# A two-layer mixture-of-experts block on one core: a new order ahead of the first step, tanh in place of exp and sigmoid, and an in-SBUF copy of the first mixing matrices

## The chip, the cores and the metric

One NeuronCore of a Trainium2 chip runs the whole program. The metric is the device time of one execution in microseconds (us); the median of three executions of the kernel before is 399.89 us (398.08 to 400.11). The engines are named PE (TensorE, matmuls), ACT (ScalarE), DVE (VectorE), POOL (GpSimd) and SP (SyncE, which here only issues transfers).

## The reference, cut to what matters

Two layers, each a mixing of the 32 channels of a sample followed by a feed-forward layer with eight low-rank experts, of which each token uses two; x is [128, 32, 512]. The first mixing is a grouped convolution of nine taps; the second is a 32x32 matrix for each sample, a softmax-weighted sum of eight matrices, where the weights come from a small network on `cond`.

```python
def _L0_ffn_ref(x, W_base, b_base, W_router, A, B):
    base = xf @ W_base.T + b_base
    rw, sel = jax.lax.top_k(xf @ W_router.T, 2)
    rw = jax.nn.softmax(rw, axis=-1)
    lora = einsum('ter,te,eor->to', einsum('td,erd->ter', xf, A), w, B) * 2.0
    return base + lora

def _L1_cond_ref(x, embedding, W0, b0, W1, b1, W2, b2, weight, bias_k):
    h = gelu(embedding @ W0 + b0); h = gelu(h @ W1 + b1)
    att = jax.nn.softmax(h @ W2 + b2, axis=-1)
    return einsum('boi,bih->boh', einsum('bk,koi->boi', att, weight), x) + att @ bias_k

x = x + _L0_ffn_ref(_L0_cond_ref(x, cond_128, ...), ...)
x = x + _L1_ffn_ref(_L1_cond_ref(x, cond_128, ...), ...)
```

## The kernel before

The 128 samples are worked on in 32 tiles of four samples, 128 tokens (sample and channel) of 512 values each. Every number that goes into a large matmul is split into a high part (`fp32r`, made by an ACT copy) and a low part (the rest, made by a subtraction on DVE or POOL), and each product is three matmuls: high x high, high x low, low x high (`SPLITS`). The weights of both layers (`wa`: experts' A, router and the first half of the base; `wb`: its second half; `lb_w`: experts' B) are loaded once and split once.

For tile t the first layer is `conv(t)` on PE, `conv_out` on DVE (adds a bias, gives `y0`), `turn0` (four transposes on PE), `turned0` on ACT and DVE (high and low parts of `yT`), `first_product(0,t)`, `choose` and `gate` on DVE with `weigh` on ACT between them (the two best experts and their weights), `turn_hw`, `second_product`, `b_product`, and `middle` on DVE, which writes `x1`. The second layer is `mix_product(t)` (PE; `x1` against `mix_part`, the split mixing matrices of the tile's four samples), `save_cross`/`sum_mixed`/`turned1`, then `first_product(1,t)` and so on, and `result` on DVE. The loop is a software pipeline: `step(t)` does the first layer of tile t, the convolution of tile t+1 and the second layer of tiles t-1 and t-2.

Nothing schedules this but the order in which the instructions of each engine are written, and semaphores between engines. Each engine has one queue in order, so an instruction that waits holds back all behind it on that engine. SP's queue of transfers works in the same way.

Ahead of `step(1)` the kernel splits weights, runs the small network (two Gelus, a softmax with exp) and makes `mix_nat`, all mixing matrices as rows of one sample each. `mix` holds them block-diagonally, four samples to a tile; the blocks are brought there by writing `mix_nat` to a scratch tensor in HBM and reading it back with four transfers (L256 to L262). PE's own order ahead of the first step is at L390 to L453. While PE waits for other engines there it runs matmuls on zeros, `keep_busy` (L384): ten at the start, and

```python
            conv(0)
            kernel_scores()
            turn0(0)
            keep_busy(4)
            turn_probabilities()
            keep_busy(2)
            mixing_setup()
            first_product(0, 0)
```

On ACT three activation tables are loaded: Gelu at the start (L495), exp for the softmax (L506), sigmoid for `weigh` (L513). ACT's order is at L495 to L507 and L585 to L601, DVE's at L814 to L832, POOL's at L903 to L920.

## Time and profile before

| | |
|---|---|
| three executions | 398.08, 399.89, 400.11 us |
| the profiled execution | 400.4 us, span 398.6 us (first to last instruction) |
| PE busy | 387.8 us, 97% of the span |
| DVE, POOL, ACT busy | 70%, 57%, 52% |
| mean granted clock of PE | 0.996 of full speed |
| chain that ended last | PE 91%, DVE 5%, DMA 1% |

The span is what the trace covers; the time of the same execution is 1.8 us longer. Shares of busy time are means over the span: the 40 us ahead of and in the first steps have other limits than the loop. The trace has for each instruction its start, its duration and, in brackets, how long its engine had stood idle before it and what ended that. PE's clock has two levels, 1.2 and 2.4 GHz; the profile gives the granted level as 0.50 or 1.00.

### The profile page before, as it was taken

What the parts mean: (1) busy time and instruction counts of PE and PEld (TensorE: products, weight loads), DVE (VectorE), ACT (ScalarE), POOL (GpSimd) and SP (SyncE); (2) the same over time, 40 slices, a digit from 0 to 9 for tenths busy, and PEclk for the clock granted to TensorE, in tenths of its full rate; (3) what the DMA queues carried; (4) which work ended last, traced back from release to release, by engine and by line L of the source; (5) the groups of instructions that cost most, each with busy time, mean ns of one, the idle gap of its engine ahead of it and who ended that gap; (6) DMA issues with size and microseconds to landing.
All of it is one profiled execution on the core that took longest, in us unless ns stands there. A gap on an engine that the chain in (4) does not pass through costs nothing.

```text
span 398.6 us, 9113 instructions
## 1 busy us (share of the span) xinstructions
PE 387.8 (97%) x2789; PEld 377.5 (95%) x2789; DVE 280.8 (70%) x982; ACT 207.8 (52%) x529; POOL 226.7 (57%) x199
## 2 busy tenths in 40 slices
PE   7979999999999999999999999999999999999985
PEld 6659999999999999999999999999999999999975
DVE  2786876777667677766777676677777767767764
ACT  3846455555455555544555555455555545555441
POOL 3386756555666555556656555665655566655550
PEclk9998999999999999999999999999999999999999
DMA  7871212122221212222112122211212222121101
GB/s 257 297 142 55 76 31 81 56 79 79 79 79 38 68 57 75 79 79 79 54 52 70 62 79 79 79 59 47 79 53 79 79 79 77 37 72 53 56 27 54
DMA packets 19677, 31.04 MB, mean 78 GB/s; under 512 B 5904, under 2 KB 5936, under 8 KB 19664
## 3 DMA queue, kind: packets, MB, share of 16 engines
q1 hardware_dynamic: 19664, 30.89, 25.1%
q8 instruction: 6, 0.10, 0.1%
q14 instruction: 7, 0.06, 0.0%
...
## 4 chain that ended last, share of the span: by engine, by line
PE 91%; DVE 5%; DMA 1%; issue 1%; ACT 0%; POOL 0%; SPq 0%; DVEq 0%; ACTq 0%
PE ps_out L331 33%; PE ps_out L343 22%; PE ps_conv L299 11%; PE ps_out L363 11%; PE ps_mix L377 5%; PE ps_t L311 3%; PE ps_mix L380 2%; DMA pack<-in_pack 1%; PE ps_t L350 1%; DVE wb L625 1%; DVE yT L625 1%; PE ps_out L350 1%; DVE y L774 1%; DVE lb_w L641 0%; DVE x L767 0%
## 5 line engine op out<-in xcount | busy, mean ns | idle before, releaser
L331 PE MATMUL ps_out<-wa,yT 128*128 128x392 f32 x768 | 152.5, 345 | 1.4 <-ACT yT L476 0.7
L331 PEld LDWEIGHTS ps_out<-wa,yT 128*128 128x128 f32 x768 | 132.2, 188 | 4.8 <-DVE yT L625 1.8
L879 POOL TENSOR_TENSOR x_part<-x,x_part 128x512 fp32r<-128x512 f32 x31 | 40.1, 1295 | 116.4 <-ACT x_part L476 116.4
L343 PE MATMUL ps_out<-wb,yT 128*128 128x256 f32 x768 | 105.6, 287 | 0.2 <-DVE wb L625 0.2
L343 PEld LDWEIGHTS ps_out<-wb,yT 128*128 128x128 f32 x768 | 97.2, 191 | 0.4 <-issue 0.4
L476 ACT ACTIVATE yT<-ps_t 64x256 fp32r<-64x256 f32 x128 | 48.5, 379 | 29.3 <-PE ps_t L311 26.9
L363 PE MATMUL ps_out<-lb_w,hwT 128*128 128x256 f32 x384 | 59.5, 289 | 1.3 <-ACT hwT L476 0.7
L892 POOL TENSOR_TENSOR x1b<-x,base_bias 128x512 f32<-128x512 f32 x31 | 40.1, 1294 | 28.4 <-DVE res L752 28.4
L625 DVE TENSOR_TENSOR yT<-ps_t,yT 64x256 fp32r<-64x256 f32 x128 | 53.7, 420 | 3.0
L513 ACT ACTIVATE wts<-top 128x1 f32<-128x1 f32 x128 | 30.4, 284 | 46.5 <-DVE top L716 46.5
L299 PE MATMUL ps_conv<-x_part,conv_w 128*128 128x256 f32 x384 | 52.2, 286 | 0.0
L363 PEld LDWEIGHTS ps_out<-lb_w,hwT 128*128 128x128 f32 x384 | 49.7, 189 | 2.6 <-ACT hwT L476 1.2
L299 PEld LDWEIGHTS ps_conv<-x_part,conv_w 128*128 128x128 f32 x384 | 49.3, 192 | 0.0
L864 POOL TENSOR_TENSOR x_part<-x_raw,x_part 128x520 fp32r<-128x520 f32 x31 | 40.5, 1308 | 12.0 <-ACT x_part L476 12.0
L885 POOL TENSOR_TENSOR base_bias<-passed,bias 128x512 f32<-128x512 f32 x32 | 41.8, 1306 | 4.0 <-ACT passed L539 4.0
L875 POOL TENSOR_TENSOR xb<-x_tok,bias 128x512 f32<-128x512 f32 x32 | 41.8, 1305 | 0.0
L476 ACT ACTIVATE x_part<-x_raw 128x520 fp32r<-128x520 f32 x32 | 20.5, 640 | 34.9 <-PE ps_conv L299 34.9
L752 DVE TENSOR_TENSOR res<-ps_out,x1b 128x512 f32<-128x512 f32 x31 | 21.4, 691 | 20.5 <-PE ps_out L363 20.5
L377 PE MATMUL ps_mix<-mix_part,x_part 128*128 128x256 f32 x128 | 31.4, 323 | 1.4 <-issue 1.4
L476 ACT ACTIVATE yT<-ps_mix 128x512 fp32r<-128x512 f32 x32 | 19.1, 598 | 24.0 <-DVE ps_mix L787 23.1
L625 DVE TENSOR_TENSOR hwT<-ps_out,hwT 128x128 fp32r<-128x128 f32 x32 | 9.3, 290 | 30.6 <-ACT hwT L476 30.6
L380 PE MATMUL ps_mix<-mix_part,x_part 128*128 128x128 f32 x128 | 28.6, 224 | 0.0
...
## 6 DMA issues: line engine op xcount, KB each, us to landing
...
x_tok<-in_x_tok SPq DMA_DIRECT2D x32, 256.0 KB, 2.6
out<-res SPq DMA_DIRECT2D x31, 256.0 KB, 2.0
...
lb_raw<-in_lb SPq DMA_DIRECT2D x2, 256.0 KB, 5.8
bias<-in_bias SPq DMA_DIRECT2D x2, 256.0 KB, 5.8
...
```

Source lines behind the costliest of these rows:

```text
L299: last = mm(ps_conv[:, h * SPT * NB:(h + 1) * SPT * NB], conv_w[:, wp, h, shift, :], x_part[dp][:, h, :, shift:shift + NB], start=(n == 0 ...
L331: last = mm(out_banks(y, t)[:, 0, 0:AR + DH], yT[y][dp][:, k, :], wa[y][:, wp, k, :], start=(n == 0 and k == 0), stop=(n == len(SPLITS) - ...
L343: last = mm(out_banks(y, t)[:, 1, OUT], yT[y][dp][:, k, :], wb[y][:, wp, k, :], start=(n == 0 and k == 0), stop=False, skip_group_check=True)
L363: last = mm(out_banks(y, t)[:, half, OUT], hwT[y][dp][:, :], lb_w[y][:, wp, half * DH:(half + 1) * DH], start=False, stop=(n == len(SPLITS ...
L377: mm(ps_mix[:, b, c:c + 2 * P], x1_part[HI][:, k * P:(k + 1) * P], mix_part[:, :, :].rearrange("p a b -> p (a b)"), start=True, stop=False ...
L476: return nc.scalar.activation(dst, src, ACT.Copy)
L625: return v.tensor_tensor(dst, src, hi, ALU.subtract)
L864: g.tensor_tensor(x_part[LO][:, :, :, :], x_raw[:, :, :, :], x_part[HI][:, :, :, :].bitcast(F32), ALU.subtract).then_inc(s["xl"], 1)
L875: g.tensor_tensor(xb[:, :], x_tok[:, :], bias[0][:, :], ALU.add).then_inc(s["xb"], 1)
L879: g.tensor_tensor(x1_part[LO][:, :], x1[:, :], x1_part[HI][:, :].bitcast(F32), ALU.subtract).then_inc(s["x1l"], 1)
L885: g.tensor_tensor(base_bias[:, :], passed[:, :], bias[1][:, :], ALU.add).then_inc(s["bb"], 1)
L892: g.tensor_tensor(dst[:, :], x1[:, :], base_bias[:, :], ALU.add).then_inc(s["x1b"], 1)
```

## The change

- **PE's order.** Nine matmuls on zeros in place of ten, `conv(0)` directly behind them and ahead of the small network; the other six matmuls on zeros are gone. `turn_probabilities` stands inside `first_product(0,0)` behind its first four matmuls, `conv(1)` inside it ahead of its last four, `mixing_setup` behind it.
- **ACT's order.** `wa` of layer 0 is made in two halves around the second Gelu, `wa` of layer 1 ahead of the first `weigh`; both halves of `mix_nat` are copied by ACT (one was DVE's); `save_sums`, `pass_bias(0)`, `high_wb(1)` and `high_lb(1)` move from `step(1)` to the part ahead of it. `split_mix(0)` stands ahead of `split_x1(0)`.
- **One table.** The softmax takes e^x = 2/(1 - tanh(x/2)) - 1, so DVE has six small operations on `att` between the scores and the product with `own` where it had two and the scores' maximum. `weigh` takes 1 + tanh(x/2): a small copy `half_top` ahead of each pair, with a semaphore between, for every tile of both layers. `lb_w` takes half the scale.
- **POOL.** It subtracts the second half of layer 0's `wa` (was DVE's), and forms `xb` of tile 0 ahead of the column sums.
- **SP.** `lb0` and `x` of tile 1 are loaded ahead of `kern`, the second layer's `lb1` and `bias1` ahead of `mix_nat`. Four transfers inside SBUF bring the first tile's blocks from `mix_nat` to `mix`; then the scratch tensor is written and the other tiles' blocks are read back. ACT waits for the first four ahead of `split_mix(0)`, for the others in `step(1)`.

PE ahead of the first step, before: `ps_out<-x_part` are the matmuls on zeros, `ps_conv` the convolution, `ps_t` the transposes of `y0`, `att_m` and `att_mT` the softmax.

```order
L388 MATMUL ps_out<-x_part 128x512 x10
L393 MATMUL ps_mix<-pack 128x128
L396 MATMUL ps_mix<-pack 128x128 x2
L399 MATMUL ps_mix<-hid,pack 128x128
L299 MATMUL ps_conv<-x_part,conv_w 128x256 x12
L403 MATMUL ps_mix<-pack,hid 128x8
L311 MATMUL ps_t<-pack,y 128x128 x4
L388 MATMUL ps_out<-x_part 128x512 x4
L408 MATMUL ps_mix<-pack,att_m 32x128
L388 MATMUL ps_out<-x_part 128x512 x2
L415 MATMUL ps_mix<-att_mT,bk_sb 128x128
L418 MATMUL ps_mix<-kern_sb,att_mT 128x512
```

And in the changed kernel:

```order
L399 MATMUL ps_out<-x_part 128x512 x9
L307 MATMUL ps_conv<-x_part,conv_w 128x256 x12
L404 MATMUL ps_mix<-pack 128x128
L407 MATMUL ps_mix<-pack 128x128 x2
L410 MATMUL ps_mix<-hid,pack 128x128
L319 MATMUL ps_t<-pack,y 128x128 x4
L414 MATMUL ps_mix<-pack,hid 128x8
L342 MATMUL ps_out<-wa,yT_0 128x392 x4
L419 MATMUL ps_mix<-pack,att_m 32x128
L342 MATMUL ps_out<-wa,yT_0 128x392 x4
L307 MATMUL ps_conv<-x_part,conv_w 128x256 x12
L342 MATMUL ps_out<-wa,yT_1 128x392 x4
```

The convolution came up, four products of `first_product(0,0)` stand ahead of the softmax's transpose, and between the transposes of `y0` and `second_product` no matmul on zeros is left.

ACT ahead of the first step, before, from the first Gelu on (`hid`):

```order
L501 ACTIVATE hid<-ps_mix,pack 128x128
L503 ACTIVATE hid<-ps_mix,pack 128x128
L476 ACTIVATE wa<-wa_raw 128x1568
L506 ACT_TABLE_LOAD
L506 ACTIVATE att,att_s<-att,att_s 128x8
L476 ACTIVATE yT_0<-ps_t 64x4x64 x4
L476 ACTIVATE wb<-wb_raw 128x1024
L493 ACTIVATE lb_w<-lb_raw 128x512
L476 ACTIVATE x_part<-x_raw 128x520
L476 ACTIVATE mix_nat<-ps_out 128x512
L513 ACT_TABLE_LOAD
L513 ACTIVATE wts<-top 128x1 x2
```

And in the changed kernel:

```order
L589 ACTIVATE hid<-ps_mix,pack 128x128
L485 ACTIVATE wa<-wa_raw 128x784
L592 ACTIVATE hid<-ps_mix,pack 128x128
L485 ACTIVATE wa<-wa_raw 128x784
L485 ACTIVATE yT_0<-ps_t 64x4x64 x2
L507 ACTIVATE att<-att 128x8
L485 ACTIVATE yT_0<-ps_t 64x4x64 x2
L485 ACTIVATE x_part<-x_raw 128x520
L485 ACTIVATE wb<-wb_raw 128x1024
L502 ACTIVATE lb_w<-lb_raw 128x512
L485 ACTIVATE wa<-wa_raw 128x784 x2
L512 ACTIVATE half_top<-top 128x2
```

The two table loads behind the Gelus are gone. The softmax's operation now stands between the two pairs of `yT` copies, and no longer ahead of both.

POOL ahead of the first step, before (`k_sums`, `k_sum` are layer 1's column sums):

```order
L903 MEMSET mix 128x4096
L904 MEMSET ones 128x128
L864 ISA
L864 TENSOR_TENSOR x_part<-x_raw,x_part 128x520
L908 TENSOR_TENSOR k_sums<-wa_raw 128x2x392
L911 TENSOR_TENSOR k_sums<-wb_raw 128x2x256
L914 TENSOR_TENSOR k_sum<-k_sums 128x648
L875 TENSOR_TENSOR xb<-x_tok,bias 128x512
L879 TENSOR_TENSOR x_part<-x,x_part 128x512
L869 TENSOR_TENSOR mix_part<-mix,mix_part 128x128
```

And in the changed kernel:

```order
L925 MEMSET mix 128x4096
L926 MEMSET ones 128x128
L928 ISA
L928 TENSOR_TENSOR wa<-wa_raw,wa 128x784
L886 TENSOR_TENSOR x_part<-x_raw,x_part 128x520
L897 TENSOR_TENSOR xb<-x_tok,bias 128x512
L935 TENSOR_TENSOR k_sums<-wa_raw 128x2x392
L938 TENSOR_TENSOR k_sums<-wb_raw 128x2x256
L941 TENSOR_TENSOR k_sum<-k_sums 128x648
L891 TENSOR_TENSOR mix_part<-mix,mix_part 128x128
L901 TENSOR_TENSOR x_part<-x,x_part 128x512
```

A subtraction on half of `wa` came in at the front, `xb` moved ahead of the column sums, and `mix_part` ahead of `x_part<-x`.

The diff, cut to its core:

```diff
@@ block.sync: behind load_weights(0)
+            sp.dma_start(lb_raw[0][:, :], d["lb0"]).then_inc(l_lb[0], 16)
+            load_x(1)
             sp.dma_start(kern_sb[:, :], d["kern"]).then_inc(l_kern, 16)
             sp.dma_start(bk_sb[:, :], d["bk"]).then_inc(l_kern, 16)
...
+            sp.wait_ge(mix_zero, 1)
             sp.wait_ge(mix_nat_ready, 2)
+            for n in range(SPT):
+                sp.dma_start(mix[n * C:(n + 1) * C, n, :],
+                             mix_nat[n:n + 1, :].rearrange("p (i o) -> p i o", o=C)).then_inc(mix_first, 16)
             sp.dma_start(d["scratch"], mix_nat[:, :]).then_inc(mix_stored, 16)
-            load_x(2)
             sp.wait_ge(mix_stored, 16)
-            sp.wait_ge(mix_zero, 1)
             for j in range(SPT):
-                sp.dma_start(mix[j * C:(j + 1) * C, j::SPT, :],
-                             d["scratch"][j::SPT, :].rearrange("t (i o) -> i t o", o=C)).then_inc(mix_loaded, 16)
+                sp.dma_start(mix[j * C:(j + 1) * C, SPT + j::SPT, :],
+                             d["scratch"][SPT + j::SPT, :].rearrange("t (i o) -> i t o", o=C)).then_inc(mix_loaded, 16)
@@ block.tensor
-            keep_busy(10)
+            keep_busy(9)
+            conv(0)
...
-            conv(0)
+            turn0(0)
             kernel_scores()
-            turn0(0)
-            keep_busy(4)
-            turn_probabilities()
-            keep_busy(2)
+            first_product(0, 0, before_cross=turn_probabilities, before_low=lambda: conv(1))
             mixing_setup()
-            first_product(0, 0)
-            conv(1)
             second_product(0, 0)
@@ block.scalar
-            nc.scalar.activation(att[:, 1, :], att[:, 0, :], ACT.Exp, bias=att_s[:, 0:1],
-                                 accum_out=att_s[:, 1:2]).then_inc(mlp_act, 1)
+                act.wait_ge(mlp_dve, 3)
+                nc.scalar.activation(att[:, 2, :], att[:, 1, :], ACT.Tanh).then_inc(mlp_act, 1)
...
                 act.wait_ge(s["top"][y], t + 1)
+                nc.scalar.activation(half_top[y][:, :], top[y][:, 0:2], ACT.Copy, scale=0.5).then_inc(s["half"][y], 1)
+                act.wait_ge(s["half"][y], t + 1)
                 for k in range(2):
-                    nc.scalar.activation(wts[y][:, k:k + 1], top[y][:, 1 - k:2 - k], ACT.Sigmoid, scale=-1.0,
-                                         bias=top[y][:, k:k + 1]).then_inc(s["wts"][y], 1)
+                    nc.scalar.activation(wts[y][:, k:k + 1], top[y][:, 1 - k:2 - k], ACT.Tanh, scale=-0.5,
+                                         bias=half_top[y][:, k:k + 1]).then_inc(s["wts"][y], 1)
...
             turned0(0, 0)
+            probabilities()
             turned0(0, 1)
+            split_x(1)
             high_wb(0)
             high_lb(0)
-            split_x(1)
...
+            act.wait_ge(mix_first, 16 * SPT)
+            split_mix(0)
             split_x1(0)
-            act.wait_ge(mix_loaded, 16 * SPT)
-            split_mix(0)
+            save_sums()
+            pass_bias(0)
+            high_lb(1)
             split_x(2)
@@ block.vector: probabilities()
+                v.tensor_scalar(att[:, 1, :], att[:, 2, :], -1.0, 1.0, ALU.mult, ALU.add).then_inc(mlp_dve, 1)
...
+                v.reciprocal(att[:, 3, :], att[:, 1, :]).then_inc(mlp_dve, 1)
...
+                v.tensor_scalar(att[:, 0, :], att[:, 3, :], 2.0, -1.0, ALU.mult, ALU.add).then_inc(mlp_dve, 1)
...
+                v.tensor_reduce(att_s[:, 1:2], att[:, 0, :], AX.X, ALU.add).then_inc(mlp_dve, 1)
@@ block.gpsimd
+            pool.wait_ge(wa_hi[0], 2)
+            g.tensor_tensor(wa[0][:, LO, LAST_KS, :], wa_raw[0][:, LAST_KS, :], wa[0][:, HI, LAST_KS, :].bitcast(F32),
+                            ALU.subtract).then_inc(wa_lo[0], 1)
             split_x(1)
+            pool.wait_ge(l_bias[0], 16)
+            form_xb(0)
...
+            split_mix(0)
             split_x1(0)
-            split_mix(0)
```

## Rows read from the trace of the kernel before

**Rows 1.** Page, part 1: busy us, share of the span and instructions of each engine
```profile
PE 387.8 (97%) x2789; PEld 377.5 (95%) x2789; DVE 280.8 (70%) x982; ACT 207.8 (52%) x529; POOL 226.7 (57%) x199
```

**Rows 2.** Chain of waits in order of time, in the loop: start us, us, what
```profile
52.84 2.15 PE ps_out L331 x12
...
58.12 1.43 PE ps_conv L299 x12
...
64.39 2.14 PE ps_out L331 x12
```

**Rows 3.** Timeline, PE ahead of step 1: start us, us, instruction, count [idle before]
```profile
1.46 4.64 PE L388 MATMUL ps_out<-x_part 128*128 128x512 f32 x10 [1.46 <-DVE x_part L645]
...
6.87 0.80 PE L393 MATMUL ps_mix<-pack 128*128 128x128 f32 x2 [0.77 <-DMA pack<-in_pack]
...
8.64 2.46 PE L299 MATMUL ps_conv<-x_part,conv_w 128*128 128x256 f32 x12
...
11.95 0.66 PE L311 MATMUL ps_t<-pack,y 128*128 128x128 f32 x4 [0.73 <-DVE y L774]
...
14.13 0.48 PE L415 MATMUL ps_mix<-att_mT,bk_sb 32*128 32x128 f32 x2
...
16.27 1.70 PE L331 MATMUL ps_out<-wa,yT 128*128 128x392 f32 x8
```

**Rows 4.** Timeline, ACT ahead of step 1
```profile
10.81 1.28 ACT L506 ACT_TABLE_LOAD   x1
...
12.20 0.30 ACT L506 ACTIVATE att<-att,att_s 128x8 f32<-128x8 f32 x1
...
12.64 1.59 ACT L476 ACTIVATE yT<-ps_t 64x256 fp32r<-64x256 f32 x4
...
21.02 0.48 ACT L513 ACTIVATE wts<-top 128x1 f32<-128x1 f32 x2 [2.74 <-DVE top L716]
```

**Rows 5.** Timeline, DVE and POOL: operations with two SBUF inputs, alone and side by side
```profile
12.08 0.96 DVE L625 TENSOR_TENSOR wa<-wa_raw,wa 128x784 fp32r<-128x784 f32 x1
...
16.44 1.31 POOL L864 TENSOR_TENSOR x_part<-x_raw,x_part 128x520 fp32r<-128x520 f32 x1 [12.04 <-ACT x_part L476]
...
17.71 1.86 POOL L908 TENSOR_TENSOR k_sums<-wa_raw 128x784 f32<-128x784 f32 x1
...
18.13 2.53 DVE L625 TENSOR_TENSOR wb<-wb_raw,wb 128x1024 fp32r<-128x1024 f32 x1
```

**Rows 6.** Timeline, PE and DVE: the way to step 1
```profile
22.38 0.33 PE L350 MATMUL ps_out<-pack,hw 128*128 128x128 f32 x1
...
25.25 0.69 DVE L767 TENSOR_TENSOR x<-ps_out,xb 128x512 f32<-128x512 f32 x1 [1.04 <-POOL xb L875]
```

**Rows 7.** Timeline, SP and PE: the way to the first mixing product
```profile
19.82 2.47 SPq L261 DMA_DIRECT2D mix<-scratch  x4
...
30.04 0.36 PE L377 MATMUL ps_mix<-mix_part,x_part 128*128 128x256 f32 x1 [1.37 <-issue]
```

**Rows 8.** DMA issues: transfers, KB each, median us from issue to landing
```profile
out<-res SPq DMA_DIRECT2D x31, 256.0 KB, 2.0
...
mix<-scratch SPq DMA_DIRECT2D x4, 128.0 KB, 3.5
```

**Rows 9.** Stretches: us, busy us of each engine (x), granted clock, DMA share, GB/s
```profile
31.00:34.00 3.00, 3.00 (x16) 3.00 (x16) 1.04 (x3) 2.67 (x7) 0.74 (x2) 0.50 0.30 89
...
34.00:35.00 1.00, 1.00 (x9) 1.00 (x9) 0.52 (x1) 1.00 (x2) 1.00 (x2) 0.85 0.00 0
```

**Rows 10.** Timeline, the last tile: ACT, DVE and PE
```profile
388.50 0.60 ACT L476 ACTIVATE yT<-ps_mix 128x512 fp32r<-128x512 f32 x1 [0.94 <-PE ps_out L343]
...
392.90 0.18 DVE L731 TENSOR_TENSOR ps_out<-ps_out,wts 128x16 f32<-128x16 f32 x1
...
393.67 0.33 PE L350 MATMUL ps_t<-pack,hw 128*128 128x128 f32 x1
```

**Rows 11.** Timeline, ACT in the loop
```profile
55.24 0.48 ACT L513 ACTIVATE wts<-top 128x1 f32<-128x1 f32 x2 [1.27 <-DVE top L716]
```

158 lines of the change are left out of this document (84 added, 74 removed).

## The prediction, made before the changed kernel ran

> **What bounds the kernel now.** Start with the busy shares [rows 1]: PE is busy for 97% of the span, the next engine for 70%. So only two things make the kernel shorter: less work on PE, or fewer stretches in which PE stands still or runs at its lower clock. The chain of waits in order of time [rows 2] says where those stretches are not. From one `first_product(0,t)` to the next it takes 64.39 - 52.84 = 11.55 us, all of it PE, step after step. The change removes nothing from PE in the loop, so the loop can't gain; it can only lose. What is left is the part ahead of the loop, and the last tile. There I read the timeline, engine by engine.
>
> Four things are to be seen in it. First, PE runs at 1.2 GHz at the start: `conv(0)`, twelve matmuls, takes 2.46 us [rows 3], the same form 1.43 later [rows 2]. Second, `step(1)` begins when `x1` of tile 0 is written, at 25.25 + 0.69 = 25.94, and DVE had stood 1.04 for `xb` there [rows 6]. Third, the mixing product waits: PE is idle for 1.37 us until 30.04 [rows 7]. Fourth, right after that the granted clock stands at 0.50 (the 1.2 GHz level) from 31 to 34, and at a mean of 0.85 in the next microsecond, which is 0.3 us more [rows 9]. 3.3 us at half the clock lose 1.65 us of PE's work. The stall and the low clock together, 3.0 us, are what this change could win at most in step 1.
>
> **The sum.** It is made against the profiled execution (400.4 us, its span and 1.8 us around it), which is 0.5 above the median of the three.
>
> *Convolution first.* Nine matmuls on zeros instead of ten end at 1.46 + 0.9 x 4.64 = 5.6, and `conv(0)` starts there and not at 8.64: 3.0 earlier. But the products for its bias, which lay ahead of it (6.87 to 8.64, 1.8 us [rows 3]), now lie between it and `y0`. So the transposes of `y0`, which ended at 11.95 + 0.66 = 12.61, end some 1.2 earlier, at 11.4.
>
> *Table loads.* The two removed cost nothing. The first ended at 12.09 and its exp ran at 12.20, once DVE had the maximum; after the second ACT still stood 2.74 for `top` [rows 4]. The Trainium skill (ScalarE: Activation LUTs, "What ACT_TABLE_LOAD costs") puts each switch of table set at about 2.66 us with its drain. By that the change would win 5.3 us; the rows show 1.28 for a load, and none of it on the path.
>
> *The softmax.* This is where the change loses. DVE's operations on the scores and `wa` now meet POOL's subtraction on half of `wa`. How such a meeting goes is shown by [rows 5]: POOL's 128x784 sum ran from 17.71 to 19.57; DVE's 128x1024 subtraction, started at 18.13, ended at 20.66, which is 1.09 after POOL's end, while DVE alone takes 0.96 for 784 columns, so about 1.2 for 1024. It did nothing until POOL was done. The Trainium skill (SBUF — State Buffer, "Who interferes with whom") has this as a lock on a shared pair of ports, held for a whole instruction, and says that `tensor_scalar` can be caught as well. The first agrees with the rows; no row of before shows the second. POOL's half starts behind ACT's, at about 11, and takes 1.86: until 12.9. Then DVE subtracts its own half (0.96, to 13.9), and does five small operations at about 0.2 (an estimate: ACT's on the same 128x8 takes 0.30 [rows 4]): 14.9. The product with `own` has two SBUF inputs again and may meet `split_x(1)`, 1.31 on POOL. So `att_m` is written between 15.1 and 16.4; I take 16.0, nearer to the blocked end, as in the row of the same kind. Before, it was used by 13.5. Of the `yT` copies (1.59 [rows 4]) the second pair waits for the tanh and ends between 13.3 and 14.2, where before they ended at 14.23.
>
> *PE from there.* Behind `att_m`, PE has its transpose (0.2), eight of the first product's twelve matmuls (two thirds of 2.15), `conv(1)` 1.43, the mixing set-up (14.13 to 16.27, 2.1 [rows 3]) and the second product, as many matmuls of the same form as a convolution, 1.43: 6.6. From 16.1 that ends at 22.7, and `turn_hw` was at 22.38 [rows 6]: 0.3 late at full clock. The four products done early win 0.7, the set-up that moved behind costs that back and more.
>
> *The clock.* Between 11.4 and 16.1 PE now has about 1.0 us of work. The matmuls on zeros that filled this stretch are gone. Before, 1.37 us of idleness were followed by a fall for 3.3 us; here nearly 4 of 4.7 us are idle. I expect the fall, and for as long, in the dense work behind: 1.65. `turn_hw` is then at 24.35.
>
> *To `x1`.* Before, it took 25.94 - 22.38 = 3.56, of which 1.04 was for `xb`. That wait goes, as `xb` is formed ahead of the column sums. DVE has half of layer 1's `wa` and a pair of `yT` in front of `x1` instead, in part beside PE. Take 2.8: `x1` at 27.2, 1.2 late.
>
> *To the mixing product.* The last kernel product ends 1.43 ahead of `turn_hw`, at 22.9. ACT's last copy of `mix_nat` takes 0.60 (as its copy of the same size in [rows 10]): 23.5. Four issues took 2.47 us [rows 7], so the last goes out 1.85 after the first, at 25.4. The trace has no transfer inside SBUF; the nearest are a store with 2.0 to landing and the scratch reads with 3.5 [rows 8], whose 128-byte pieces the new ones share while they are a thirty-second of the size. I take the middle, 2.75, and keep both ends: the blocks land at 28.1 (27.4 to 28.9). Behind this wait on ACT stand `split_mix(0)` and, newly, `split_x1(0)`, and behind that POOL's low part: 0.3 + 0.6 + 1.3 = 2.2. The product starts at 30.35 (29.6 to 31.1), 0.3 late. PE's idleness ahead of it shrinks nevertheless, because `step(1)` starts late too: 27.25 + 2.15 = 29.4, so 0.95 and not 1.37. I take this as not enough for a second fall: 1.65 won.
>
> *The loop.* `half_top` adds one operation of some 0.3 us ahead of each pair of `weigh`. ACT had stood 1.27 us there [rows 11], and PE waits for nothing in the step: zero. The cover is that slack; without it each step would cost up to 0.3, 32 steps some 10 us.
>
> *The last tile.* Here nothing covers it. DVE takes the weights at 392.90, and PE turns the result at 393.67, as soon as it is there [rows 10]: 0.3 late. A tile earlier ACT's `yT` at 388.50 waited for PE as well as for the chain behind `weigh`: 0.1 more. Together 0.4.
>
> Sum: +0.3 - 1.65 + 0.4 = -0.95, so 400.4 - 0.95 = 399.45, about **399.5 us**.
>
> **The rivals.** *The clock holds in the front* (chance 0.2). For it: PE came through gaps of 0.7 there before [rows 3]. Against it: the gaps are now several times that. Then `x1` comes at about 26.0 and the product at 29.4: -0.65 - 1.65 + 0.4 = -1.9, 398.5; with DVE's small operations not blocked another 0.9, 397.6.
>
> *The clock falls again at the mixing product, and the kernel is slower* (0.2). The place is ACT's wait for the four transfers, with `split_x1(0)` queued behind it. It decides from an idle stretch of about 1.4, which is reached if landing takes 3.2 and not 2.75. Then nothing of the 1.65 is won: up to +1.1 late and +0.4, 401.9. If the low clock in the front also lasts twice as long, 1.65 more: 403.5. I put this case at 402.3.
>
> *The tables count after all* (0.05): by the skill's price per switch, 5.3 us less, 395.1. The waits behind both loads speak against it.
>
> *All of it is hidden* (0.05): DVE's queue, not PE, sets `x1` in both orders, and the late start eats what step 1 wins: 400.4.
>
> **How the numbers follow.** My forecast has 0.5 and by its own bounds (landing 2.0 to 3.5, `att_m` 15.1 to 16.4) reaches from 398.5 to 400.8. About 0.5%, 2.0 us, can be told from no change here, so faster means below 397.9, slower above 401.9. Faster: a third of the first rival, the table rival, and a tail of my own: 0.17. Slower: somewhat over half of the second rival, and a tail: 0.14. Between: 0.69. The range from 397.5 to 402.5 leaves out the ends of both large rivals and the tables, 0.15 or so.
>
> **What would show it.** Right: one table load in ACT's rows; PE mostly idle between 11.5 and 16, and a granted clock of 0.50 behind that; DVE's `att` or `wa` rows longer than alone, ending after a POOL row; an idle stretch under 1.2 ahead of the mixing product, and 1.00 from 30 to 36; 11.55 per step; `turn_hw` of the last tile 0.3 later behind `top` than before. Wrong: a granted clock of 1.00 from 12 to 24, `att_m` before 14, or the four blocks landing within 3 us of `mix_nat` with PE waiting all the same.

## The result, and the profile after

The changed kernel took **400.39 us** (median of 20 executions, 399.01 to 401.47), the kernel before, beside it, 398.61 (20 executions, 397.33 to 400.33). The ratio is 1.0039, with a 95% interval from 1.0027 to 1.0050: 1.1 to 2.0 us slower. That is inside the predicted range and under the 0.5% that I had called no change, but it is on the other side: I had forecast 0.4 less than the median shown and 0.95 less than the profiled execution.

One thing has to be known before the two traces are compared. The profiled execution of before, 400.40, is longer than each of the 20 just named; the profiled one of after, 399.01, is the shortest of its 20. So the two traces say 1.4 us faster where the times say 1.6 slower. Each step below is therefore read in several traces of each kernel.

Page of the changed kernel, part 1, which answers to [rows 1]: ScalarE has gained 11 us (two more `half_top` operations per step), PE has lost 4. One table load is left of three.

```profile
PE 383.9 (97%) x2782; PEld 374.5 (94%) x2782; DVE 281.2 (71%) x986; ACT 218.8 (55%) x593; POOL 226.8 (57%) x200
```

Timeline of the changed kernel, PE from the convolution to the first mixing product (start us, us, instruction, count [idle before]), which answers to [rows 3, 6, 7]:

```profile
5.11 1.72 PE L307 MATMUL ps_conv<-x_part,conv_w 128*128 128x256 f32 x12
...
8.92 0.66 PE L319 MATMUL ps_t<-pack,y 128*128 128x128 f32 x4 [0.86 <-DVE y L796]
...
13.51 1.65 PE L342 MATMUL ps_out<-wa,yT 128*128 128x392 f32 x4 [3.44 <-ACT yT L485]
15.51 0.40 PE L419 MATMUL ps_mix<-pack,att_m 128*32 128x128 f32 x1 [0.35 <-DVE att_m L694]
...
23.49 0.27 PE L361 MATMUL ps_out<-pack,hw 128*128 128x128 f32 x1
...
27.36 2.41 PE L342 MATMUL ps_out<-wa,yT 128*128 128x392 f32 x12 [1.07 <-DVE x L789]
29.61 0.28 PE L388 MATMUL ps_mix<-mix_part,x_part 128*128 128x256 f32 x1
```

The 3.44 us gap at 10 to 13.5 is where the fillers had been. The mixing product has no idle time ahead of it any more (1.37 in [rows 7]), and the stretch from 31 to 34 has its full clock, where [rows 9] had 0.50. The low clock lies ahead of step 1 instead, and not only here: the 42 executions of the changed kernel in this document all have a mean granted clock of 0.989 to 0.995. Stretches of the changed kernel (us, busy us of PE, PEld, DVE, ACT, POOL, granted clock, DMA share, GB/s):

```profile
11.00:18.00 7.00, 4.14 (x14) 3.65 (x15) 6.67 (x14) 4.71 (x9) 5.18 (x4) 0.53 1.01 366
18.00:19.00 1.00, 1.00 (x9) 1.00 (x8) 1.00 (x1) 0.00 (x0) 1.00 (x2) 0.85 0.80 273
31.00:34.00 3.00, 3.00 (x25) 2.98 (x24) 1.98 (x6) 1.57 (x5) 3.00 (x3) 1.00 1.00 130
```

DVE's small operations of the softmax, timeline of the same kernel. The first `tensor_scalar` on `att` took 1.81 and ended with POOL's half of `wa` (10.45 + 1.83); the second, alone, took 0.16. `att_m` was held in the same way by `split_x(1)` on POOL at 14.10.

```profile
10.50 1.81 DVE L678 TENSOR_SCALAR att<-att,att_s 128x8 f32<-128x8 f32 x1
12.23 0.96 DVE L641 TENSOR_TENSOR wa<-wa_raw,wa 128x784 fp32r<-128x784 f32 x1
13.11 0.16 DVE L684 TENSOR_SCALAR att<-att 128x8 f32<-128x8 f32 x1
...
14.14 1.31 DVE L694 SCALAR_TENSOR_TENSOR att_m<-att,att_s,pack 128x32 f32<-128x32 f32 x1
```

The table that the rest is read from is worked out from the timelines: the start of the first mixing product, the intervals from the first matmul of one mixing product to that of the next (step 1, step 2, and the mean of 26 in the loop), what follows the last of the 32, the span, and the time around the span. The lines below the second are executions of the experiments.

| trace | first mixing product | step 1 | step 2 | loop | after the last | span | around it |
|---|---|---|---|---|---|---|---|
| before, profiled | 30.0 | 12.83 | 11.96 | 11.545 | 12.8 | 398.6 | 1.8 |
| after, profiled | 29.6 | 11.72 | 12.21 | 11.532 | 13.0 | 397.2 | 1.8 |
| c_before | 29.6 | 11.48 | 11.95 | 11.544 | 12.8 | 396.8 | 1.8 |
| c_after | 29.2 | 11.73 | 12.18 | 11.533 | 13.1 | 396.9 | 2.5 |
| c_after2 | 30.9 | 11.72 | 12.16 | 11.533 | 13.1 | 398.5 | 2.7 |
| e_nohalf | 30.0 | 10.75 | 12.01 | 11.533 | 13.6 | 397.0 | 1.8 |
| e_wadve | 28.8 | 11.70 | 12.16 | 11.533 | 13.1 | 396.4 | 2.4 |
| e_bhold | 31.2 | 11.48 | 11.96 | 11.544 | 12.9 | 398.5 | 1.9 |

### The profile page after: what moved, and what is told of

Same layout as the page of the kernel before. It is cut to its first block, busy times and chain, and to the rows that moved or that the text cites. A ratio compares the mean times of both kernels' runs of the same rounds, so it can differ in the third digit from the quotient of the medians.

```text
span 397.2 us, 9172 instructions
## 1 busy us (share of the span) xinstructions
PE 383.9 (97%) x2782; PEld 374.5 (94%) x2782; DVE 281.2 (71%) x986; ACT 218.8 (55%) x593; POOL 226.8 (57%) x200
## 4 chain that ended last, share of the span: by engine, by line
PE 88%; DVE 5%; ACT 2%; issue 2%; DMA 2%; POOL 0%; SPq 0%; DVEq 0%; ACTq 0%
PE ps_out L342 33%; PE ps_out L354 21%; PE ps_conv L307 11%; PE ps_out L374 11%; PE ps_mix L388 5%; PE ps_t L319 3%; PE ps_mix L391 2%; DMA wa_raw<-in_wa 2%; PE ps_t L361 1%; PE ps_out L361 1%; DVE yT L641 1%; DVE x L789 1%; ACT yT L485 0%; DVE att L678 0%; DVE lb_w L653 0%
## 5 line engine op out<-in xcount | busy, mean ns | idle before, releaser
L354 PE MATMUL ps_out<-wb,yT 128*128 128x256 f32 x768 | 104.2, 285 | 0.0
L354 PEld LDWEIGHTS ps_out<-wb,yT 128*128 128x128 f32 x768 | 95.8, 189 | 0.8 <-issue 0.8
L485 ACT ACTIVATE yT<-ps_t 64x256 fp32r<-64x256 f32 x128 | 48.5, 379 | 28.4 <-PE ps_t L319 26.0
L914 POOL TENSOR_TENSOR x1b<-x,base_bias 128x512 f32<-128x512 f32 x31 | 40.1, 1295 | 27.8 <-DVE res L774 27.8
L512 ACT ACTIVATE half_top<-top 128x2 f32<-128x2 f32 x64 | 12.5, 195 | 36.7 <-DVE top L738 36.7
L515 ACT ACTIVATE wts<-top,half_top 128x1 f32<-128x1 f32 x128 | 30.7, 287 | 2.1
L388 PE MATMUL ps_mix<-mix_part,x_part 128*128 128x256 f32 x128 | 31.2, 321 | 0.0
```

The lines of the kernel that those rows point to most:

```text
L354: last = mm(out_banks(y, t)[:, 1, OUT], yT[y][dp][:, k, :], wb[y][:, wp, k, :], start=(n == 0 and k == 0), stop=False, skip_group_check=True)
L388: mm(ps_mix[:, b, c:c + 2 * P], x1_part[HI][:, k * P:(k + 1) * P], mix_part[:, :, :].rearrange("p a b -> p (a b)"), start=True, stop=False ...
L485: return nc.scalar.activation(dst, src, ACT.Copy)
L914: g.tensor_tensor(dst[:, :], x1[:, :], base_bias[:, :], ALU.add).then_inc(s["x1b"], 1)
```

## The experiments

### Both kernels once more

`c_before` is the kernel before, `c_after` and `c_after2` are the changed one, with no edit.

> The kernel before, unchanged, to have span and granted clock of each of its executions. Theory A (the clock: before loses 1.65 us to a low clock in step 1 in part of its executions only, the change loses to a low clock in its front in every one): the executions fall into two groups some 1.7 apart, the longer ones with a mean granted clock of about 0.996 and the shorter ones with 1.000. Rival B (before's spread has nothing to do with the clock): clock the same in long and short executions. Rival C (the loss of the change lies outside the span): time less span is 1.8 in all executions here, where the change has 1.8 to 3.1.

> The changed kernel unchanged, beside the kernel before on the same chip. Theory A (the measured +1.6 us is the kernel's own): span near 398.0 with the low clock of the front in every execution (mean granted clock 0.989 to 0.994), and a time outside the span that varies between 1.8 and 3.0 with a median near 2.5, against 1.8 for the kernel before; ratio 1.003 to 1.005. Rival B (the +1.6 us came of the chip or the sample): span and time within 0.5 us of the kernel before, time outside the span 1.8.

> The changed kernel unchanged, once more on the chip of this call. Theory A: time outside the span 1.8 to 3.0 with a median above 2.1, median span 397.5 to 398.1, ratio to the kernel before 1.002 to 1.006; in its trace the low clock lies ahead of step 1 and the first two steps take 11.7 and 12.2 us. Rival B (the first two traces were of short executions and are not typical): a span near 398.0 with one of the first two steps longer by 0.5 us or more, or the front.

Measured: `c_before` 398.44, ratio 0.9997 [0.9981, 1.0013]; `c_after` 399.99, ratio 1.0039 [1.0023, 1.0056]; `c_after2` 400.54, ratio 1.0036 [1.0017, 1.0054]. The loss is the kernel's own, and it has two parts. On the chip of `c_after2` the mean span was 398.14 against 397.03 for the kernel before (1.1), and the time around the span 2.39 against 1.80 (0.6); on the chip of `c_after` 397.82 against 397.08, and 2.34 against 1.80.

`c_before` also shows what the profiled execution of before had hidden. Timeline of `c_before`, PE, and the stretch from 31 to 34:

```profile
29.60 0.36 PE L377 MATMUL ps_mix<-mix_part,x_part 128*128 128x256 f32 x1 [1.37 <-issue]
```

```profile
31.00:34.00 3.00, 3.00 (x25) 3.00 (x25) 1.43 (x3) 2.97 (x7) 1.10 (x1) 1.00 0.34 89
```

The stall is the same 1.37 us as in [rows 7]. The clock after it stayed at 1.00, and step 1 took 11.48, not 12.83. So the fall cost 1.35 us where it happened.

Of the theories for `c_before`, C held: the time around the span was 1.76 to 1.84 in all twelve executions. A held in part. Beside `c_before`, `c_after`, `c_after2` and `e_bhold` 117 executions of the kernel before can be compared, and in 60 of these its mean granted clock was 0.996 or less. These 60 had spans longer by 0.6, 1.2, 1.2 and 1.2 us in the mean than the others of the same chip, but the two groups overlap. Where the low clock lay in them is not shown, since only one execution of a run has a trace.

`c_after2` shows a longer front. Timeline, PE, and stretches:

```profile
5.46 2.42 PE L307 MATMUL ps_conv<-x_part,conv_w 128*128 128x256 f32 x12
...
13.65 1.25 PE L342 MATMUL ps_out<-wa,yT 128*128 128x392 f32 x4 [2.89 <-ACT yT L485]
...
24.74 0.27 PE L361 MATMUL ps_out<-pack,hw 128*128 128x128 f32 x1
...
30.87 0.28 PE L388 MATMUL ps_mix<-mix_part,x_part 128*128 128x256 f32 x1
```

```profile
11.00:14.00 3.00, 0.35 (x2) 0.38 (x3) 2.86 (x7) 1.87 (x6) 1.43 (x1) 1.00 1.05 338
14.00:21.00 7.00, 6.26 (x25) 5.42 (x23) 6.14 (x10) 3.24 (x5) 6.67 (x5) 0.51 0.68 244
```

In the profiled execution the low clock began at about 11 and ran in part over the gap, where PE had nothing to do. Here it began at 14, when the gap was over, and fell on work throughout: `turn_hw` 24.74 instead of 23.49, for the same low clock of some 7 us. Its length differs too. In `c_after`, stretches:

```profile
11.00:13.60 2.60, 0.00 (x0) 0.00 (x0) 2.56 (x4) 1.22 (x5) 1.49 (x1) 1.00 1.08 319
13.60:17.00 3.40, 2.94 (x9) 2.45 (x10) 3.17 (x9) 3.16 (x5) 2.69 (x3) 0.50 0.99 396
17.00:18.00 1.00, 1.00 (x10) 1.00 (x9) 0.94 (x3) 0.54 (x1) 1.00 (x1) 0.98 0.93 345
```

There it was 3.4 us, and the first mixing product came at 29.2. Mean granted clocks of 0.994 or 0.995, as in this execution, are rare: 4 of the 42. Where the low clock begins and how long it lasts differs from one execution to the next.

### The clock's fall in step 1 of the kernel before, alone

`e_bhold` fills PE's 1.37 us stall of step 1 in the kernel before.

```
                 first_product(0, t)
+                if isinstance(t, int) and t == 1:
+                    pe.wait_ge(s["x1h"], 1)
+                    for _ in range(6):
+                        mm(ps_mix[:, 0, :], x1_part[HI][:, 0:P], x1_part[HI][:, :], start=True, stop=True)
                 mix_product(t - 1)
```

> The kernel before with six filler products in step 1 of the loop, where TensorE waits for the low half of x1 (1.37 us idle ahead of the first mixing product), nothing else. This takes out by itself the fall of the clock that the prediction priced at 1.65 us. Theory A (that fall is what separates the longer executions of the kernel before, some 1.5 us longer and a third of them, from the shorter ones): the first step takes 11.5 us and the clock stays at 1.00 from step 1 on in the trace, the long executions vanish, the median span falls by 0.2 to 0.5 and the mean by 0.4 to 0.7. Rival B (the fall is only one cause among several, or fillers cost what they save): median and mean within 0.2 of the kernel before, long executions as frequent as there.

Measured: 398.69, ratio 0.9994 [0.9977, 1.0012], between 0.9 us won and 0.5 lost. Step 1 took 11.48 in its trace, and the fillers delay nothing: the first mixing product starts 4.05 us behind the first matmul of `first_product` in this trace as in `c_before`. The 1.65 us that I took for this fall are outside that interval, and so are the 1.35 that it cost in the one trace, so not every execution of the kernel before can pay them. Three of twelve executions still had spans of 397.7 and more (9 of 24 of the kernel before, beside it), and 5 of 12 a mean granted clock of 0.996 or less (14 of 24). So longer ones have other causes too, low clocks elsewhere among them: in the trace of `e_bhold` the first mixing product came at 31.2, and the granted clock had been 0.50 from 9 to 12.

### The front: fillers, and POOL's half of `wa`

`e_fill` puts fillers back into the changed kernel's gaps. `e_wadve` gives POOL's half of `wa` to DVE, behind the softmax.

```
             kernel_scores()
+            keep_busy(14, 1)
+            def filled_turn():
+                keep_busy(4, 1)
+                turn_probabilities()
-            first_product(0, 0, before_cross=turn_probabilities, before_low=lambda: conv(1))
+            first_product(0, 0, before_cross=filled_turn, before_low=lambda: conv(1))
```

```
             probabilities()
+            low_wa_part(0, LAST_KS, 2)
             turned0(0, 0)
...
-            pool.wait_ge(wa_hi[0], 2)
-            g.tensor_tensor(wa[0][:, LO, LAST_KS, :], wa_raw[0][:, LAST_KS, :], wa[0][:, HI, LAST_KS, :].bitcast(F32),
-                            ALU.subtract).then_inc(wa_lo[0], 1)
```

> The changed kernel with matmuls on zeros again in the two idle stretches of PE in its front (14 ahead of the first product, 4 ahead of the softmax's transpose, into a bank that is free then). Theory A: granted clock 1.00 from 10 to 20, and the work from 15.5 to 19.0 about 1.1 us shorter, so step 1 begins near 26.3 and not 27.36, and the median is about 1.0 below the changed kernel's 400.4. Rival (DVE's queue with POOL's operations in it sets the start of step 1, not PE): step 1 begins within 0.3 of 27.36 though the clock holds, and the time is the same as the changed kernel's.

> The changed kernel with the second half of wa's low part on DVE again, behind the softmax's product, and not on POOL. Theory of the shared ports: DVE's tensor_scalar on att takes 0.16 and not 1.81, the tanh runs near 11.0 and not 12.35, the first product begins near 12.2 and not 13.5, att_m comes 1 to 2 us earlier. What that is worth in time depends on the clock: with a fall as now, 0 to 1.0 less than the changed kernel; without a fall, 1 to 2 less. Rival (tensor_scalar was long for another reason): it stays at 1.8.

Measured: `e_fill` 399.09, ratio 0.9998 [0.9981, 1.0016]; `e_wadve` 398.57, ratio 0.9996 [0.9978, 1.0014]. Against the changed kernel's 1.0036 to 1.0039 each wins about 0.4%, 1.6 us, and each stops level with the kernel before. But they win it in different places. The mean span of `e_wadve` is 396.49, 0.7 below the kernel before on its chip, where the changed kernel's is 0.7 to 1.1 above (on two other chips); its time around the span stays at 2.30. So by these means the half of `wa` on POOL costs 1.4 to 1.8 us, more than the whole loss of the span: the rest of the new order wins something that this one move takes away. The mean span of `e_fill` is 397.58, 0.4 above the kernel before, and its time around the span is 1.79. So the fillers win only 0.3 to 0.7 in the span; the other 0.55 or so are had without any filling, as `e_pad` shows below, since 18 matmuls are also 36 instructions.

In the trace of `e_fill` the clock was 1.00 throughout the front, and the first mixing product came at 28.4 and not at 29.6. But step 1 then took 14.94. Timeline of `e_fill`, ACT and PE in step 1:

```profile
35.27 0.31 ACT L491 ACTIVATE mix_part<-mix 128x128 fp32r<-128x128 f32 x1 [3.09 <-DMA mix<-scratch]
...
37.37 1.06 PE L374 MATMUL ps_out<-lb_w,hwT 128*128 128x256 f32 x6 [2.11 <-ACT hwT L491]
```

ACT stood for the remaining mixing matrices with `turn_hw`'s copy queued behind, and PE waited for that. The store to the scratch tensor took 5.0 us here from its issue to the next one; in all the other traces 2.6 to 3.5. So this execution is an unlucky one (its span, 398.7, is the second longest of its twelve), but the place is real: what the front wins, this chain can take.

In `e_wadve` DVE's operations were free. Timeline, DVE and POOL:

```profile
11.08 0.23 DVE L678 TENSOR_SCALAR att<-att,att_s 128x8 f32<-128x8 f32 x1
...
13.15 0.25 DVE L694 SCALAR_TENSOR_TENSOR att_m<-att,att_s,pack 128x32 f32<-128x32 f32 x1
```

```profile
13.39 2.05 POOL L887 TENSOR_TENSOR x_part<-x_raw,x_part 128x520 fp32r<-128x520 f32 x1 [9.00 <-ACT x_part L485]
```

1.81 became 0.23 and 1.31 became 0.25, and now POOL stood: 2.05 for a split that takes 1.30 alone. The low clock stayed (0.50 from 12 to 18). First mixing product 28.8.

### `half_top` left out

`e_nohalf` drops the halving and its wait; the tanh takes `top` itself as bias, so the expert weights come out with other values.

```
-                nc.scalar.activation(half_top[y][:, :], top[y][:, 0:2], ACT.Copy, scale=0.5).then_inc(s["half"][y], 1)
-                act.wait_ge(s["half"][y], t + 1)
...
-                                         bias=half_top[y][:, k:k + 1]).then_inc(s["wts"][y], 1)
+                                         bias=top[y][:, k:k + 1]).then_inc(s["wts"][y], 1)
```

> The changed kernel without the copy half_top and its wait; the two tanh take top itself as bias, so the experts' weights are other numbers, at the same cost. Theory: half_top costs only in the last tile: 0.3 to 0.4 less than the changed kernel, about 400.0. Rival (half_top costs in the loop too): the distance between two first products in the loop falls below 11.53, and the time by more than 1 us. Rival (a little later weights cost nothing): no difference.

Measured: 398.79, ratio 0.9996 [0.9979, 1.0013]. One operation of 0.2 us per pair of weights costs about 1.6 us here. By the table, the loop is not the place (11.533 with and without). Step 2 is: 12.01 against 12.16 to 12.21, where DVE stood 0.36 for `wts` on the way to hw. The last tile is: `turn_hw` came 1.46 behind the start of the last second product, as before (1.45), against 1.67 in the changed kernel (its final store landed 0.8 later in this one execution, hence the 13.6). And step 1 is, by a race. Timeline of the changed kernel, then of `e_nohalf`:

```profile
34.41 1.30 POOL L914 TENSOR_TENSOR x1b<-x,base_bias 128x512 f32<-128x512 f32 x1
34.48 2.32 DVE L641 TENSOR_TENSOR wb<-wb_raw,wb 128x1024 fp32r<-128x1024 f32 x1
...
35.36 0.26 ACT L485 ACTIVATE hwT<-ps_out 128x128 fp32r<-128x128 f32 x1
...
36.72 0.28 DVE L641 TENSOR_TENSOR hwT<-ps_out,hwT 128x128 fp32r<-128x128 f32 x1
```

```profile
34.63 1.29 DVE L639 TENSOR_TENSOR wb<-wb_raw,wb 128x1024 fp32r<-128x1024 f32 x1
...
34.80 2.26 POOL L912 TENSOR_TENSOR x1b<-x,base_bias 128x512 f32<-128x512 f32 x1
...
35.64 0.26 ACT L485 ACTIVATE hwT<-ps_out 128x128 fp32r<-128x128 f32 x1
...
35.94 0.29 DVE L639 TENSOR_TENSOR hwT<-ps_out,hwT 128x128 fp32r<-128x128 f32 x1
```

Here whoever starts first runs alone (1.30, 1.29), the other stands until it is done (2.32, 2.26). In the changed kernel POOL was 0.07 us ahead, DVE lost 1.0 us, and hw with it; PE stood 0.49 for hw. Without `half_top` DVE was ahead. Counted from the first mixing product, POOL starts at the same time in both (4.80 and 4.81 us behind it) and DVE at 4.87 and 4.64, so it is the 0.2 us of `half_top` that decide; in `c_after` and `c_after2` POOL is ahead by 0.07 and 0.05. Of the 1.6 us, 0.4 are less time around the span (mean 1.95 against 2.34 and 2.39). The rest lies in the span, mean 396.82, 0.35 below the kernel before on its chip; in its trace the race (0.97 of step 1) is most of that.

### Step 1: one wait taken away at a time

`e_mixlate` puts ACT's wait for the scratch loads behind hw and the x tile. `e_wbearly` converts layer 1's `wb` ahead of step 1.

```
                 turned1(t - 1)
-                if isinstance(t, int) and t == 1:
-                    act.wait_ge(mix_loaded, 16 * SPT)
+                first = isinstance(t, int) and t == 1
+                if first:
+                    turned_hw(0, t)
+                    split_x(t + 2)
+                    act.wait_ge(mix_loaded, 16 * SPT)
                 split_mix(t)
```

```
             high_wa_part(1, LAST_KS)
+            high_wb(1)
             weigh(0, 0)
...
             low_lb(0)
+            low_wb(1)
             turned_hw(0, 0)
```

> The changed kernel with ScalarE's order in step 1 turned round: it turns hw of step 1 and splits the third x tile first, and waits for the scratch loads of the mixing matrices and splits tile 1's after that. Theory A (step 1 holds the lost time: ScalarE stands in its queue for the scratch round trip, whose landing varies from one execution to the next, and hw waits behind it): the step from the first mixing product to the second goes from 11.72 us in the changed kernel's profile to 11.2 or less, and the median span falls by 0.4 to 1.0 against the changed kernel on the same chip. Rival B (VectorE's blocked low half of the second expert's weights, 2.32 us, sets hw's time, not ScalarE): the step stays at 11.6 to 11.8 and the median within 0.3.

> The changed kernel with the second expert's second weights converted ahead of step 1: ScalarE's high half in its idle time ahead of the gate weights (3.13 us idle there), VectorE's low half in its idle time ahead of turned hw (1.23 us idle there), instead of 1.05 us ahead of the turned y on ScalarE and 2.32 us in step 1 on VectorE. Theory A (the first step of the changed kernel is long because VectorE stands in that blocked subtraction and hw waits behind it): the first mixing product starts at 28.6 to 29.2 (29.6), the step to the second one takes 11.2 or less (11.72), the span is 0.7 to 1.5 us shorter. Rival B (another wait is next, the x tile's load or the transposes of y): the first step keeps 11.6 to 11.8, the span is at most 0.5 shorter.

Measured: `e_mixlate` 400.11, ratio 1.0037 [1.0019, 1.0056], step 1 11.70; `e_wbearly` 400.08, ratio 1.0037 [1.0016, 1.0058], step 1 11.64. My theory fell in both. Two waits end side by side. Without ACT's, DVE's subtraction still took 2.31 and hw's low half came at 36.32; without DVE's, ACT stood 1.77 for the mixing matrices and 0.49 for the x tile, and hw's low half came at 36.74.

### The copies inside SBUF undone

`e_scratch` sends the first tile's mixing matrices through the scratch tensor with the others, and waits for all of them ahead of `split_mix(0)`.

```
-            for n in range(SPT):
-                sp.dma_start(mix[n * C:(n + 1) * C, n, :],
-                             mix_nat[n:n + 1, :].rearrange("p (i o) -> p i o", o=C)).then_inc(mix_first, 16)
...
-            act.wait_ge(mix_first, 16 * SPT)
+            act.wait_ge(mix_loaded, 16 * SPT)
```

> The changed kernel with the copies of the first tile's mixing matrices inside SBUF undone: all mixing matrices go through the scratch tensor, as in the kernel before, everything else as changed. Theory A (the copies take a round trip of some 5 us off the way to step 1 and so pay for their issue): the scratch loads land at about 30, the first mixing product starts at 32 to 33 where the changed kernel has 29.6, the time is 2.5 to 5 us longer than the changed kernel's. Rival B (the gain of the copies is given back in step 1, which waits for the same round trip): the first mixing product is late by 2 to 3 us, but the second one by less than 1, and the time within 1 us of the changed kernel's.

Measured: 405.62, ratio 1.0179 [1.0154, 1.0204]: 5.6 us above `c_after`, more than the 2.5 to 5 expected. Timeline, ACT and PE, and a stretch:

```profile
31.11 0.31 ACT L481 ACTIVATE mix_part<-mix 128x128 fp32r<-128x128 f32 x1 [4.59 <-DMA mix<-scratch]
...
33.43 0.55 PE L384 MATMUL ps_mix<-mix_part,x_part 128*128 128x256 f32 x1 [3.61 <-POOL x_part L895]
```

```profile
34.00:37.00 3.00, 3.00 (x16) 3.00 (x16) 1.34 (x4) 1.94 (x7) 2.39 (x2) 0.50 0.09 5
```

PE stood for 3.6 us, and the granted clock was 0.50 from 33 to 40. In the new order of work the copies are needed. In the changed kernel their issue ran from 22.74 to 25.25 and ACT read the blocks at 26.52 without waiting.

### The time around the span

`e_bnofill` takes the six later fillers (4 and 2) out of the kernel before. `e_pad` adds 18 products of 8 columns to the changed kernel's gap.

```
             kernel_scores()
+            for _ in range(18):
+                mm(ps_out[1][:, 0, 0:E], x1_part[HI][:, 0:P], x1_part[HI][:, 0:E], start=True, stop=True)
             first_product(0, 0, before_cross=turn_probabilities, before_low=lambda: conv(1))
```

> The kernel before without its six filler products between the condition network and the mixing set-up, nothing else changed. Theory A (the time outside the span and the low clock of the changed kernel both come from an idle TensorE in the front): the granted clock falls to 0.50 somewhere between 12 and 22 us, mean clock 0.99 or less, time outside the span 2.0 to 3.0 in most executions, and the time is 1 to 2.5 us above the kernel before. Rival B (they come from something else the change does): time outside the span 1.8, and the time within 0.7 us of the kernel before.

> The changed kernel with 18 products of 8 columns each on TensorE, into a bank that is written anew later, in its 3.44 us gap ahead of the first product: 36 more instructions (weights and product) and some 0.6 us of work, too little to alter the front. Theory A (the time outside the span grows because TensorE's last 16 KB of instructions are fetched after its last recorded instruction, which the traces of 2.1 to 2.5 us outside show and those of 1.8 us do not; how many instructions lie ahead decides when that fetch is asked for): time outside the span 1.75 to 1.95 in every execution, the last fetch some 7 us ahead of the end, the span as in the changed kernel (median 397.6 to 398.1), the time 0.4 to 0.7 us shorter than the changed kernel's on this chip. Rival B (the low clock in the front, or something of the other engines, makes it): time outside the span varies from 1.8 to 3.0 as before, median above 2.1.

Measured: `e_bnofill` 401.89, ratio 1.0082 [1.0060, 1.0104], mean clock 0.984 to 0.991; the time around the span 1.75 to 1.83 in four of six executions and 2.12 in two. `e_pad` 399.61, ratio 1.0026 [1.0004, 1.0047]; around the span 1.78 to 1.91 in every execution, while in `c_after2`, on the same chip, it was 1.98 to 2.69. The low clock is still there in `e_pad` (mean 0.991 to 0.995). So the low clock doesn't make the longer time around the span, and 36 more instructions on PE take it away. What it is can be seen in the DMA queues. The changed kernel as profiled (1.8 us around the span) between 385 and 397, then `c_after` (2.5) from 397, where its last instruction has run at 396.9 (queue, kind: packets, MB, share of 16 engines):

```profile
q8 instruction: 1, 0.02, 0.5%
```

```profile
q8 instruction: 1, 0.02, 1.2%
```

It is the last 16 KB block of instructions. In all traces with 1.8 to 1.9 us it starts 3 to 9 us ahead of the end. In `c_after`, `e_wadve`, `e_bnofill`, `e_scratch`, `e_wbearly` and `c_after2`, with 2.1 to 2.7, it starts 1.2 to 1.8 us after the last recorded instruction (in `e_mixlate`, with 2.1, the trace ends without it). In these six the time around the span is 0.24 or 0.25 us shorter than the way from the last recorded instruction to the end of this transfer, so the two go together; that the execution isn't over before the block has landed is inferred from this. Whose instructions the block holds is not shown: `e_nohalf`, which takes instructions from ACT and none from PE, shortens the time around the span too. The Trainium skill (Runtime: NRT & Kernel Launch, "Instruction fetch mechanics") has such blocks of 256 instructions fetched by the engine's own queue while the one before runs, and calls a crossing mostly hidden; the 16 KB agree, and at the end of this program it is not hidden. `e_bnofill`, 1.0082, also shows that fillers are worth some 3 us in the old order.

### Several edits at once

`e_best` is `e_fill`, `e_wadve` and `e_wbearly` together. `e_best3` is `e_fill`, `e_wadve`, `e_mixlate`, and `x1` of tile 0 ahead of the turned y on DVE; `e_best2` is that with `wb` of layer 1 converted as the last thing ahead of step 1.

```
             low_wa_part(1, FIRST_KS, 1)
+            middle(0)
             turned0(1, 0)
-            middle(0)
             turned0(1, 1)
```

> The changed kernel with three edits: fillers on TensorE in the front's gaps (14 and 4), the low half of the first weights' second part on VectorE, the second expert's second weights converted ahead of step 1. Theory A (what the changed kernel lost lies in the front's low clock, in VectorE's blocked operations and in the time outside the span, and each can be had back by itself): first mixing product at 27 to 28, no low clock ahead of step 1, time outside the span 1.8, time 2.5 to 4 us below the changed kernel and 1 to 2.5 below the kernel before. Rival B (the round trip of the mixing matrices through the scratch tensor then sets the first step): the first step takes 12.5 us or more, TensorE idles over 1 us in it, and the time is within 0.7 of the kernel before.

> The changed kernel with four edits: fillers in the front (14 and 4), the low half of the first weights' second part on VectorE, ScalarE's wait for the scratch loads behind its turned hw in step 1, and on VectorE x1 of the first tile ahead of the turned y of the second. Theory A (the front's low clock, VectorE's order ahead of step 1 and the time outside the span are what the changed kernel lost): first mixing product at 26.8 to 27.8, first two steps 23.0 to 24.0 together, outside 1.8, time 395.5 to 397.5, which is 1.5 to 3 below the kernel before. Rival B (the scratch round trip and the x load behind it set step 1 whenever the front is early): the first step takes 12.5 or more and the time is within 0.7 of the kernel before.

> The same four edits, and the second expert's second weights converted ahead of step 1: the high half in ScalarE's idle time, the low half on VectorE as the last thing ahead of step 1. Theory A (VectorE's blocked subtraction in step 1 still costs in the first step): first step 0.4 to 0.9 shorter than without this edit and the time 0.3 to 0.9 shorter. Rival B (it blocks VectorE ahead of the first gate instead, so the first step stays or grows): time within 0.3 of the version without it, or longer.

Measured: `e_best` 398.98, ratio 1.0008 [0.9990, 1.0026], its first mixing product at 29.6 and step 1 10.82, so neither of its theories held; `e_best3` 398.32, ratio 0.9986 [0.9968, 1.0003]; `e_best2` 401.02, ratio 1.0055 [1.0030, 1.0080]. `e_best3` has the lowest time of all, though its interval overlaps that of `e_wadve` alone; it is some 2 us under the changed kernel, and by its interval between 1.3 us below the kernel before and level with it. It missed my 395.5 to 397.5. The first two steps took 23.4 together, as expected, but the first mixing product came at 30.1 and not at 26.8 to 27.8. `first_product` of step 1 started at 26.32, but then the queue of the second rival was there: ACT stood 0.95 for the four blocks with `split_x1(0)` behind, POOL's split of them took 1.21 (0.45 in the changed kernel) beside DVE's `wa`, and PE stood 1.41. Timeline of `e_best3`, ACT, POOL and PE, then of `e_best2`, PE:

```profile
27.13 0.31 ACT L491 ACTIVATE mix_part<-mix 128x128 fp32r<-128x128 f32 x1 [0.95 <-DMA mix<-mix_nat]
```

```profile
27.52 1.21 POOL L902 TENSOR_TENSOR mix_part<-mix,mix_part 128x128 fp32r<-128x128 f32 x1 [4.14 <-ACT mix_part L491]
```

```profile
30.10 0.36 PE L388 MATMUL ps_mix<-mix_part,x_part 128*128 128x256 f32 x1 [1.41 <-POOL x_part L912]
```

```profile
30.90 0.55 PE L388 MATMUL ps_mix<-mix_part,x_part 128*128 128x256 f32 x1 [2.64 <-POOL x_part L911]
```

One more subtraction on DVE ahead of step 1 made POOL's split of `x1` 2.25 long (1.26 in `e_best3`) and PE's wait 2.64. The granted clock was 0.50 from 30.4 to 37.3, where `e_best3` had 1.00 throughout behind its wait of 1.41, and 2.7 us were lost.

## Why the prediction was wrong, point by point

**The sum's base, and "1.65 won" in step 1: the step that failed.** The sum was made against one execution that had paid the fall of the clock, and the fall was credited as a gain of the change. With the same 1.37 us stall `c_before` had no fall, and `e_bhold` shows that taking the fall out alone moves the time by -0.2 us, by no more than 0.9. So this term was sized at 1.65 and measures about 0.2; even between the two profiled executions step 1 shrank by 1.11 only. The forecast of a median has to be made against a typical execution: `c_before`'s span, 396.8, not 398.6. Without the credit the sum says 0.7 us longer, and the mean spans were longer by 0.7 and 1.1; the rest of the loss lies outside the span.

Nearly all the signs that I had named for being right came: the low clock ahead of step 1, DVE's blocked operations, no idle stretch ahead of the mixing product, 1.00 from 30 to 36, the loop unchanged. None of them tested the base, and so the direction was missed with the signs in place.

**The span itself** came near, by luck. From 398.6 my sum gave 397.65; the spans of the changed kernel had medians of 397.85 to 398.2 in three sets of executions. The base was too long by about as much as the credit was too large, and the two cancel. The same luck put the time inside the range. The terms behind it:

- *Convolution first*: `conv(0)` took 1.72 (2.42 in `c_after2`) against 2.46 in [rows 3]; in `c_before` it took 1.68 in its old place. The granted clock reads 1.00 there in all of these, so the rows don't show the 1.2 GHz that I read into 2.46. And the transposes ended at 9.58 (10.64), not 11.4. It won nothing, since PE then stood for 3.44 us, for the turned y of ACT, which had the tanh ahead of it.
- *The softmax*: right in kind. `att_m` was written at 15.45, inside 15.1 to 16.4. The Trainium skill (SBUF — State Buffer, "Who interferes with whom") says that `tensor_scalar` can be caught by POOL's lock; I had no row for it, and 1.81 against 0.23 in `e_wadve` shows it.
- *The clock in the front*: right in place, 0.50 ahead of step 1, but in most executions twice as long, some 7 us and not 3.3 (3.4 in `c_after`). What it costs depends on where it begins: `turn_hw` 23.49 or 24.74, predicted 24.35. `x1` was written at 27.31 or 28.55, predicted 27.2.
- *The four blocks*: 1.8 us to landing (the row below, from the DMA issues of the changed kernel: transfers, KB each, median us), under the lower bound of my 2.0 to 3.5, and ACT read them at 26.52 without a wait. The mixing product followed the first product directly, 0.7 us sooner than my 30.35 in the profiled execution and 0.5 later in `c_after2`. The second rival had the right sign by another way: the product didn't wait, and the clock didn't fall there.

```profile
mix<-mix_nat SPq DMA_DIRECT2D x4, 4.0 KB, 1.8
```

- *The loop*: zero predicted, 0.012 us per step won, 0.3 in all. Which edit wins it I didn't try.
- *`half_top`*: zero in the loop held, 0.4 in the last tile was 0.25 to 0.35. Missing was what lies between: step 2 (0.2) and step 1, where 0.2 us decide whether POOL or DVE starts first. Leaving it out is worth about 1.6 us.
- *The tables*: no run tries them alone. A gain of 5.3 us, worked out from the price in the Trainium skill (ScalarE: Activation LUTs, "What ACT_TABLE_LOAD costs"), shows nowhere: the changed kernel is slower. From the end of ACT's operation before the first load to the start of the exp it was 1.41 us in the profiled execution of before and 1.32 in `c_before`, not 2.66.

**The time around the span**, 1.8, was taken as fixed. It grew by 0.5 to 0.6 in the mean, over a third of the loss, and `e_pad` takes it back.

**What makes up the loss.** From `c_before` to `c_after2`, rows of the table: front +1.3, step 1 +0.2, step 2 +0.2, loop -0.3, last tile +0.3; together 1.7, as the spans (398.5 - 396.8). Both spans lie near the median of their kernel on their chips (396.65 of the twelve of `c_before`, 397.1 of the 35 beside them, and 398.2). With the time around the span the two traces differ by 2.5, the mean times on that chip by 1.7: `c_after2`'s trace is of one of its longer executions. The front is what varies. In the other two traces of the changed kernel, which are short ones, it gives 0.0 and -0.4 against `c_before`; the four other rows give 0.4 to 0.5 in all three. Of the front's share, the half of `wa` on POOL is what the experiments show (`e_wadve`); its share and the others don't simply add up, since `e_wadve` and `e_nohalf` each win more than the whole loss of the span. `e_wadve` with the 36 instructions of `e_pad` was not tried.

Open is what makes the clock in the front begin to fall at 11 in one execution and at 14 in another, and last 3.4 us or 7, and how often each start happens; a trace shows only one execution.
